# A twelve-step perceiver kernel: masks turned by GpSimd, semaphores cleared by SyncE, a mask row made earlier, a norm's power issued first

## The reference

```python
# layer 0: 16 heads of 16 channels over 4096 context tokens
scores = where(mask_BxSxS2 == 0, -1e9, q @ k.T / 4); attn = softmax(scores) * group_prob...; x += (attn @ v) @ Wo
x += taylor_attention(norm(x)); x += expert_choice_of_one(norm(x))
# layer 1: the same cross attention with the same mask, then
x += frame_attention(norm(norm(x)))      # 16 heads of 64, block-causal over frames of 64
x += experts_choose_tokens(norm(x))      # each of 8 experts takes its 32 best tokens
# layer 2: cross attention with a mask of keys (1 x 4096, a bool), plain attention, 8 experts by zones
# layer 3: cross attention without a mask, a gated recurrence, a feed-forward
```

## Time and profile before

| what | us |
|---|---|
| median of 3 runs (lowest to highest) | 1602.1 (1601.02 to 1603.36) |
| the profiled execution: its own time | 1599.94 |
| its span | 1598.0 |
| TensorE, VectorE, ScalarE, GpSimd busy | 1451.5, 992.6, 713.4, 384.8 |

### The profile page before, as it was taken

How to read it: one execution, slowest core, us unless ns; L and a number is a source line. 1 busy time by engine, 2 the same in 40 slices (tenths; PEclk the granted TensorE clock), 3 DMA queues, 4 the chain that set the end, 5 groups by cost and what they waited for, 6 DMA issues and landing times. The chain is left out here.

```text
span 1598.0 us, 29795 instructions
## 1 busy us (share of the span) xinstructions
PE 1451.5 (91%) x11197; PEld 845.2 (53%) x11296; DVE 992.6 (62%) x2290; ACT 713.4 (45%) x964; POOL 384.8 (24%) x548
## 2 busy tenths in 40 slices
PE   8899997999999988599999888499999896999987
PEld 3665653555555555255555464235555582555555
DVE  4544446888888744677777233298886235888842
ACT  4144130444444431166565442146767221667662
POOL 4543141666666620100000021111100001011000
PEclk9999997999999997799999999789999997999999
DMA  8888993434336043254552196146667611566700
GB/s 263 250 268 247 274 302 117 61 61 61 61 61 153 2 73 47 50 83 74 84 85 36 35 283 211 50 68 100 90 100 212 100 19 43 80 98 92 142 19 7
DMA packets 130377, 178.22 MB, mean 112 GB/s; under 512 B 14109, under 2 KB 105269, under 8 KB 123062
## 3 DMA queue, kind: packets, MB, share of 16 engines
q1 hardware_dynamic: 117802, 161.10, 47.7%
q10 hardware_dynamic: 12432, 15.21, 2.9%
HBM read 132.44 MB, written 43.78 MB: 110 GB/s over the span
## 5 line engine op out<-in xcount | busy, mean ns | idle before, releaser
L808 ACT ACTIVATE prob_a<-ps 128x1024 f32<-128x1024 f32 x512 | 505.2, 1023 | 304.3 <-PE ps L693 193.0
L676 PE MATMUL ps<-kop,qop 116*128 116x512 bf16 x1024 | 341.9, 404 | 57.1 <-PEq L529 33.3
L821 DVE CUSTOM_DVE_ANT_0 dump_a<-ps,neg_q 128x512 bf16<-128x512 f32 (+1 forms) x485 | 328.7, 717 | 98.5 <-PE ps L676 97.0
L690 PE MATMUL ps<-qop,kop 116*128 116x256 bf16 x2048 | 349.3, 274 | 10.2 <-ACT prob_a L808 4.9
L825 DVE TENSOR_REDUCE best_a<-ps 128x1 f32<-128x512 f32 (+1 forms) x488 | 312.6, 709 | 59.0 <-PE ps L676 58.9
L690 PEld LDWEIGHTS ps<-qop,kop 116*128 116x128 bf16 x2048 | 195.2, 100 | 137.3 <-ACT prob_a L808 18.0
L676 PEld LDWEIGHTS ps<-kop,qop 116*128 116x128 bf16 x1024 | 86.9, 100 | 216.8 <-issue 95.8
L715 PE MATMUL ps<-prob_a,vop_a 128*32 128x256 f32 x3072 | 185.0, 382 | 0.0
L920 POOL TENSOR_TENSOR used_a<-prob_a,gT 128x1024 f32<-128x1024 f32 x64 | 151.3, 2364 | 87.5 <-DVE used_a L838 67.4
L693 PE MATMUL ps<-neg_k,identb 128*128 128x512 bf16 x425 | 161.8, 381 | 0.0
L899 POOL CAST mpart_a<-nmax_a 128x2 bf16<-128x2 f32 x64 | 25.3, 396 | 560.1 <-DVE nmax_a L830 560.1
(11 more groups left out here) (309 smaller groups left out, 1296.4 us busy)
## 6 DMA issues: line engine op xcount, KB each, us to landing
kop<-kparts SPq DMA_DIRECT2D x448, 128.0 KB, 5.2
kparts<-kp SPq DMA_DIRECT2D x64, 384.0 KB, 4.5
vals<-vst SPq DMA_DIRECT2D x16, 1024.0 KB, 7.0
vraw<-vals SPq DMA_DIRECT2D x64, 256.0 KB, 6.4
e_w<-in_e_w SPq DMA_DIRECT2D x6, 2048.0 KB, 16.1
z_w<-in_z_w SPq DMA_DIRECT2D x24, 256.0 KB, 7.2
ctxT<-in_ctxT SPq DMA_DIRECT2D x8, 512.0 KB, 8.0
raw<-in_mask ACTq DMA_DIRECT2D x8, 512.0 KB, 5.9
```

The costliest lines, as they stand in the source:

```text
L676: return pe.matmul(out, qop[0:R_ALL, h, t * P:(t + 1) * P], kop[0:R_ALL, h % UNROLL, j * CHUNK:(j + 1) * CHUNK], start=True, stop=True)
L690: ins = pe.matmul(st_bank(n)[:, j * NT:(j + 1) * NT], kop[0:R_ALL, h % UNROLL, k * P:(k + 1) * P], qop[0:R_ALL, h, :], start=(j % 2 == 0), ...
L808: act.activation(prob[:, n % NP, :], st_bank(n), ACT.Exp).then_inc(S("exp_done"), 1)
L821: dve.tensor_tensor_reduce(out=dump[:, k % 2, 0:width], in0=bank, in1=c.neg_q[:, t, j * CHUNK:j * CHUNK + width], scale=1.0, scalar=-3.0e3 ...
```

## The change

Four edits. The semaphores of every stage are cleared by SyncE. In the projection the masks are turned by GpSimd, in eight pieces a layer of 128 x 512, with two buffers; ScalarE keeps one load ahead of the turns, and the ones in kop are filled between the turns of layers 0 and 1. The key mask's row is loaded, made and stored in the frames stage, and `queries` of layer 2 keeps only the copy of ones into qop, issued before q is split. In the choosing stage GpSimd's power comes before `place`, and the first round reads the scores without a second copy.

```diff
--- before.py
+++ after.py
@@ -70,7 +70,7 @@
         for sem in self.made.values():
-            self.nc.gpsimd.sem_clear(sem)
+            self.nc.sync.sem_clear(sem)
             self.nc.release_semaphore(sem)
@@ -261,8 +261,9 @@
     NV = KT // VB
-    PIECE = KEYS // LAYERS
-    PIECES = 2 * QT
+    PIECE = CHUNK
+    SHARE = KEYS // LAYERS
+    PIECES = 2 * QT * SHARE // PIECE
     SLOTS, RESTS = 5, 2
@@ -280,7 +281,7 @@
         vst = sb("vst", [P, 2, H, VB, HD], F32)
-        raw = sb("raw", [P, PIECE], I32)
+        raw = sb("raw", [P, 2, PIECE], I32)
         q = QueryParts(c, 0, c.gT[:, KT - 4:KT - 2, :].rearrange("p k q -> p (k q)"),
@@ -290,12 +291,13 @@
-            raw_i = raw[:, :]
-            if i < QT:
-                cols = slice(PIECE * l, PIECE * (l + 1))
-                return c.a["mask"][i * P:(i + 1) * P, cols], raw_i, c.neg_q[:, i, cols]
+            raw_i = raw[:, i % 2, :]
+            if i < PIECES // 2:
+                t, at = i % QT, SHARE * l + PIECE * (i // QT)
+                cols = slice(at, at + PIECE)
+                return c.a["mask"][t * P:(t + 1) * P, cols], raw_i, c.neg_q[:, t, cols]
             n = PIECE // NT
-            first = QT * n * l + n * (i - QT)
+            first = SHARE // P * l + n * (i - PIECES // 2)
             tiles_k = slice(first, first + n)
@@ -432,11 +434,11 @@
                         piece = PIECES * l + i
-                        if piece >= 1:
-                            act.wait_ge(S("mask_made"), piece)
+                        if piece >= 2:
+                            act.wait_ge(S("mask_made"), piece - 1)
                         src, dst, _ = mask_piece(l, i)
-                        act.dma_start(dst, src).then_inc(S("mask_loaded"), 16)
-                        if i == 0:
+                        act.dma_start(dst, src).then_inc(S(f"mask_loaded{i % 2}"), 16)
+                        if i == 1:
                             g_share = slice(KT // LAYERS * l, KT // LAYERS * (l + 1))
@@ -469,11 +471,6 @@
                                       bv[:, l % 2, :].rearrange("p (h e) -> p h e", h=H), ALU.add).then_inc(S("v_staged"), 1)
-                    if k % VB == VB - 1:
-                        i = k // VB
-                        dve.wait_ge(S("mask_loaded"), 16 * (PIECES * l + i + 1))
-                        _, src, dst = mask_piece(l, i)
-                        dve.tensor_scalar(dst, src, -1.0, -NEG, ALU.add, ALU.mult).then_inc(S("mask_made"), 1)
@@ -497,9 +494,15 @@
                     fill_constants(c, pool, S)
-                    for u in range(UNROLL):
+                for i in range(PIECES):
+                    pool.wait_ge(S(f"mask_loaded{i % 2}"), 16 * (PIECES // 2 * l + i // 2 + 1))
+                    _, src, dst = mask_piece(l, i)
+                    pool.tensor_scalar(dst, src, -1.0, -NEG, ALU.add, ALU.mult).then_inc(S("mask_made"), 1)
+                    pool.wait_ge(S("mask_made"), PIECES * l + i + 1)
+                    if l < 2 and i % 4 == 1:
+                        u = 2 * l + i // 4
                         pool.memset(c.ops.kop[96:P, u, :], 1.0).then_inc(S("kop_ones"), 1)
-                    pool.wait_ge(S("kop_ones"), UNROLL)
+                        pool.wait_ge(S("kop_ones"), u + 1)
@@ -532,8 +535,6 @@
         qp = sb("qp", [P, 3, CT * NT], BF16)
-        raw8 = sb("raw8", [1, KEYS], U8) if l == KEYED else None
-        neg_row = sb("neg_row", [1, KEYS], BF16) if l == KEYED else None
         block = ctx.enter_context(nc.Block())
@@ -551,10 +552,6 @@
             norm_pool(c, pool, S)
-            if l == KEYED:
-                pool.wait_ge(S("keymask_loaded"), 16)
-                pool.wait_ge(S("norm_rstd"), 1)
-                pool.tensor_scalar(neg_row[:, :], raw8[:, :], -1.0, -NEG, ALU.add, ALU.mult).then_inc(S("neg_made"), 1)
@@ -580,23 +577,19 @@
         def _(sp):
+            sp.wait_ge(S("qop_set"), 1)
             if l == KEYED:
-                sp.dma_start(raw8[:, :], c.a["mask_keys"]).then_inc(S("keymask_loaded"), 16)
+                sp.dma_start(c.qop[R_MASK:R_MASK + 1, :, :], c.ops.kop[R_MAX:R_MAX + 1, 0, :]
+                             .rearrange("o (h q) -> o h q", h=H)).then_inc(S("mask_placed"), 16)
             sp.wait_ge(S("q_split"), 1)
...
             sp.wait_ge(S("q_stored"), 48)
-            sp.wait_ge(S("qop_set"), 1)
             c.ops.load_q(sp, c.ops.S("q_first"), slice(0, UNROLL))
+            c.ops.load_q(sp, c.ops.S("q_rest"), slice(UNROLL, H))
             if l == KEYED:
-                sp.dma_start(c.qop[R_MASK:R_MASK + 1, :, :], c.ops.kop[R_MAX:R_MAX + 1, 0, :]
-                             .rearrange("o (h q) -> o h q", h=H)).then_inc(S("mask_placed"), 16)
-                sp.wait_ge(S("neg_made"), 1)
-                sp.dma_start(c.ops.kop[R_MASK:R_MASK + 1, :, :],
-                             neg_row[0:1, :].unsqueeze(1).to_broadcast((1, UNROLL, KEYS))).then_inc(S("mask_placed"), 16)
-                sp.wait_ge(S("mask_placed"), 32)
-            c.ops.load_q(sp, c.ops.S("q_rest"), slice(UNROLL, H))
+                sp.wait_ge(S("mask_placed"), 16)
@@ -1335,6 +1328,8 @@
         oT = sb("oT", [P, M, NT], F32)
+        raw8 = sb("raw8", [1, KEYS], U8)
+        neg_row = sb("neg_row", [1, KEYS], BF16)
         block = ctx.enter_context(nc.Block())
@@ -1348,8 +1343,13 @@
             sp.dma_start(wo[:, :, :], tiles(c.a["m_wo"])).then_inc(S("wo"), 16)
+            sp.dma_start(raw8[:, :], c.a["mask_keys"]).then_inc(S("keymask_loaded"), 16)
             load_next(sp)
-            c.ops.load_first(sp, 2)
+            c.ops.load_first(sp, KEYED)
+            sp.wait_ge(S("neg_made"), 1)
+            sp.dma_start(c.ops.kop[R_MASK:R_MASK + 1, :, :],
+                         neg_row[0:1, :].unsqueeze(1).to_broadcast((1, UNROLL, KEYS))).then_inc(S("mask_placed"), 16)
+            sp.wait_ge(S("mask_placed"), 16)
@@ -1359,6 +1359,10 @@
             add_bias_pool(c, pool, S, bo)
+            pool.wait_ge(S("bias_added"), 1)
+            pool.wait_ge(S("keymask_loaded"), 16)
+            pool.tensor_scalar(neg_row[:, :], raw8[:, :], -1.0, -NEG, ALU.add, ALU.mult).then_inc(S("neg_made"), 1)
+            pool.wait_ge(S("neg_made"), 1)
             for m in range(M):
@@ -1674,7 +1678,7 @@
         score = sb("score", [E, NT], F32)
-        left = sb("left", [E, ROUNDS + 1, NT], F32)
+        left = sb("left", [E, ROUNDS, NT], F32)
         top = sb("top", [E, ROUNDS, 8], F32)
@@ -1709,13 +1713,13 @@
+            norm_pool(c, pool, S)
             pool.iota(place_i[:, :], pattern=[[1, PLACES]], base=1, channel_multiplier=0).then_inc(S("placing"), 1)
...
             pool.wait_ge(S("place"), 1)
-            norm_pool(c, pool, S)
@@ -1818,14 +1822,14 @@
             link(dve.tensor_copy(score[:, :], c.ps[0:E, 7, 0:NT]))
-            link(dve.tensor_copy(left[:, 0, :], score[:, :]))
             for r in range(ROUNDS):
-                link(dve.max(top[:, r, :], left[:, r, :]))
+                still = score[:, :] if r == 0 else left[:, r - 1, :]
+                link(dve.max(top[:, r, :], still))
                 if r == 0:
                     dve.tensor_scalar(ntop[:, :], top[:, 0, 0:1], -1.0, None, ALU.mult).then_inc(S("top_found"), 1)
-                link(dve.match_replace(out=left[:, r + 1, :], in_to_replace=top[:, r, :], in_values=left[:, r, :],
+                link(dve.match_replace(out=left[:, r, :], in_to_replace=top[:, r, :], in_values=still,
                                        imm_value=TAKEN))
-            dve.tensor_scalar(taken[:, :], left[:, ROUNDS, :], 0.9 * TAKEN, None, ALU.is_lt).then_inc(S("taken_found"), 1)
+            dve.tensor_scalar(taken[:, :], left[:, ROUNDS - 1, :], 0.9 * TAKEN, None, ALU.is_lt).then_inc(S("taken_found"), 1)
             dve.wait_ge(S("taken_found"), 1)
```

## The result

The changed kernel took 1585.14 us (1582.48 to 1586.53, 4 runs) beside 1601.56 us before (1598.51 to 1603.36, 4 runs) on the same chip: ratio 0.9897 (0.9877 to 0.9918). The pair was timed twice more: 0.9936 (0.9918 to 0.9953) and 0.9919 (0.9906 to 0.9931). Over the three, 16 runs of the changed kernel have a median of 1586.4 us, and the 68 runs of the kernel before that stand beside it and beside the experiments, on several chips, have 1599.9: 13.4 us between them, where my sum said 12.3. One execution of the kernel before, at a mean granted clock of 0.55, took 2490 us and is in none of these numbers.

A forecast was written before the change was run, and what follows sets the result against it. TensorE, busy 91% of the span, was taken as the bound, so only its waits count; -3.6 - 1.7 + 0.3 + 1.4 + 0.5 - 9.9 + 0.7 = -12.3 us, 1602.1 to 1589.8, range 1585.5 to 1594.5.

The forecast's parts named there:

- (1): Projection, masks to GpSimd: TensorE's stall in layer 0's value stage and the half clock behind it go, gain 3.6 us.
- (3): Choosing stage: norm and picks 1.55 us sooner, but the last w2 load lands late behind SyncE's clears; +0.5 us.
- in layers 1 to 3 the vals store ends the wait before and after: 0: Projection's value stages: VectorE waits for the vals store with or without the change, so no gain there, 0 us.
- I take the landings as unchanged: Projection: mask loads in halves, two in flight, leave the DMA landing times as they were; +-1.5 us for contention.
- rival B: Projection: the masks' round trips on GpSimd become the bound; up to +47 us, 1637; chance 0.05.
- (2): Clears on SyncE: norms' transposes move to 3.45 us from stage start, -1.7 us; frames +0.3, output store +1.4.
- rival A: All stages: a clear costs SyncE only 20 to 40 ns; at 30 ns 2.7 us lower, 1587.1; chance 0.2.
- D: Norms: TensorE's idle matmuls, not the clears, held them; 1.7 us less gain, 1591.5; chance 0.07.
- (4): Mask row out of queries(2): -9.9 us there, +0.7 in the attention behind it, 0 in frames.
- rival C: Frames pays 3.7, or vals stores land 1 us later per layer, or attention 2 takes 1.4 or more; +5, 1595; 0.13.

The follow-up runs named there:

- fill13: The changed kernel with 13 instead of 16 idle matmuls before each norm's transposes; ratio to the kernel before 0.9895.
- warm5: The changed kernel with 5 idle matmuls more in the choosing stage, before the picks; ratio to the kernel before 0.9929.
- act_clears: The changed kernel with the semaphores cleared by ScalarE instead of SyncE; ratio to the kernel before 0.9932.
- split: The changed kernel with 5 idle matmuls before the picks, and ScalarE clearing semaphores of frames, the last feed-forward and its weights; 1581.94 us, ratio 0.9886.
- lean: warm5 with 13 instead of 16 idle matmuls before the norms' transposes and 22 instead of 28 behind the router; ratio to the kernel before 0.9933.
- best: split with 13 instead of 16 idle matmuls before the norms' transposes, but 16 in the frames stage; ratio to the kernel before 0.9893.
- row_only: The kernel before with the key mask row made in frames instead of queries(2), and the qop row copied before q is split; ratio 0.9957.
- double_clears: The changed kernel with every semaphore cleared twice on SyncE; 1592.97 us, ratio to the kernel before 0.9966.

## Where the prediction was wrong, and where it was right

The direction was right and the time fell just outside the range. The step that failed is in (1): a term put at 0, because the landings of the stores were taken as unchanged. The cause given for (3) was wrong too, though its number was near.

**(1) Masks: the step "in layers 1 to 3 the vals store ends the wait before and after: 0" failed.** The store does end VectorE's wait before and after, as the step says. What failed is the 0, and "I take the landings as unchanged" behind it: in layer 1 the store lands 1.3 us sooner on average, TensorE's stall goes, and the stage is 1.0 us shorter. In layer 3 it lands 1.3 us sooner too, and the stage is 1.7 us shorter in the means of a varying stage; there three of the five profiles with the masks on VectorE also show a stall of 0.65 to 0.87 us of TensorE right behind VectorE's wait for a mask piece. Layer 0 was right in place, and 0.9 us too large (2.7 for 3.6, by the means). Together 5.2 us for 3.6 in the profiles. The times do not bear it out alike: without the masks' part the change loses 2 to 8 us, but the masks' part alone gives 0.8 us (-2.6 to +1.1). On GpSimd a piece takes 0.62 us (I took 0.7), and rival B had no part: layers 1 to 3 did not get longer by more than 0.2 us. The Trainium skill (SBUF — State Buffer, SBUF: two separate sides) has a VectorE operation shut out by GpSimd when it has two SBUF inputs and GpSimd reads SBUF, or when it runs in a 2-port mode; this eviction has one input in PSUM. The trace agrees: the value stage's tensor_tensor has a mean of 423 ns with the masks on GpSimd and 421 without.

**(2) Clears.** The powers stand 0.25 us behind each variance and the transposes 3.45 us from each start, as forecast: queries(3) to the first score is 0.89 us shorter (0.9). A clear costs SyncE 57 to 70 ns, where I took 70: rival A, 20 to 40 ns, was wrong. So was D: with the clears off GpSimd all transposes that had stood later than 3.45 us from their start came sooner, by as much as the steps said (0.13 to 1.25 us; taylor, plain attention and the last stage stood at 3.45 before too), and only then do the idle matmuls hold them, as fill13 shows. At the store +1.14 (I had +1.4), in frames +0.2 (+0.3). The row with attention 1 has +0.4 instead of -0.4. Its queries gained 0.2 of the 0.4 us, the attention gave that back, and 0.39 us more lie between the last add behind the attention and the next statistics, where no engine has a row. They are there in all 12 profiles with the masks on GpSimd and in none of the five without, so they belong to the masks' edit and not to the clears; their cause is open.

**(3) Choosing: right number, wrong cause.** +0.3 for +0.5, but the last w2 load was not what TensorE waited for. SyncE's first issue came 1.97 us behind VectorE's first instruction (2.5 forecast), and the last load landed 28.04 us behind the variance, 0.4 ahead of the second half that needs it. What took the gain was the clock, which fell behind the 1.18 us gap that came sooner. warm5, act_clears and split show both bounds and in which order they stand. That the number came out near was luck. Why the clock falls there when the chain is early and not when it is late is open; shown is only that filling the gap keeps it full, in four profiles of four (warm5, lean, split, best). Half of the edit, the copy dropped, gave nothing at all: TensorE's 28 idle matmuls behind the router end 1.4 us after `taken` is known, and took 6.15 us before and after.

**(4) The mask row.** -9.9 in queries(2) (25.55 to 15.71 us from variance to score, -9.84) and +0.7 in the attention behind, -9.2 together as measured. The frames stage hid the row: it starts at 925.81, and GpSimd is idle for 7.5 us behind it. The first two parts of rival C had no part. Its third, attention 2 taking the whole 1.4 us, is seen in row_only (1.5) and in one of the changed kernel's three profiles (1.4; 0.3 in the others); my 0.7 is the mean of the three.

**The range.** The sum was 12.3, the pooled difference 13.4; the 1.1 between is of the size of the masks' missing term (1.6 in the profiles). The first comparison gave 16.4 us, and most of what lies above 13.4 is spread: I took 2.4 us from three runs of the kernel before, while its 68 runs go from 1594.2 to 1606.4 and the changed kernel's 16 from 1582.5 to 1591.0. The medians of 4 to 6 runs of the changed kernel give 16.4, 11.5 and 13.4 us for one and the same change. So that the first time fell 0.36 us outside is in part chance; with either of the other two it would have been inside. What makes single executions differ is seen only in part (the clock in frames and in taylor, the landings in layer 3) and stays open.

## What to carry to other kernels

When two engines' instructions collide, ask of every other edit whether it moves one of the two in time: here a change of the clears alone undid a collision for which a step of its own had been written. Where a stage's gain is missing, read the granted clock in the gaps that now come sooner before you blame the load that would be late next; both may hold it, and then the first repair shows nothing. Take a term at 0 only when you have asked what else moves on its path: a store that ended the wait before and after landed 1.3 us sooner with the masks' part changed. Clears of semaphores cost least on the engine whose first work in the next stage comes last; split placed those of three stages so, and its profile has the two stages behind them 2.7 us shorter.

## What was not expected of the hardware

A gap of 1.18 us in TensorE's work that came 0.7 to 1.8 us sooner, with the same work between the transposes and it, was followed by a fall of the granted clock from 1.00 to 0.50 for 3.4 us (6.8 in one), in nine profiles of nine. A wait of 2.19 us for a DMA cost 3.9 us in double_clears, since the matmuls behind it ran at nearly half speed; one of 1.15 us in warm5 cost only itself. SyncE's price of a semaphore clear (57 to 70 ns) is GpSimd's (71 to 72 ns) or a little less.
